# An LSTM with a sign-weight FFN: x's last quarter and Wx as scaled pairs of f16

## The chip, the cores and the metric

The kernel runs on one core of a Trainium2 chip. The metric is the device time of one execution in microseconds (us), the median of three runs.

## What is computed

An LSTM over 64 steps with 32 sequences and 256 features, and a three-layer network whose weights are only +1 or -1, on all 2048 outputs of the LSTM, added to x:

```python
xW = einsum('ntd,dg->ntg', x, Wx) + b          # x: 32 x 64 x 256, Wx: 256 x 1024
def step(h, c, xw_t):                          # 64 times
    a = xw_t + h @ Wh                          # 32 x 1024
    i, f, o = sigmoid(three quarters of a); g = tanh(last quarter)
    c = f * c + i * g
    h = o * tanh(c)
z = concatenate([hs, -hs], -1)                 # 2048 x 512
z = relu(s0 * z @ W0) * 2                      # W0: 512 x 1024 of +1/-1
z = relu(s1 * z @ W1) * 2                      # W1: 1024 x 1024 of +1/-1
out = x + s2 * z @ W2                          # W2: 1024 x 256 of +1/-1
```

## The kernel before

**Number formats.** A product of two fp32 operands is made from halves. For x @ Wx each operand is split into a value rounded to the matmul's rounded fp32 and the rest (`xs`, `wxs`), and three of the four products are summed: 6 matmuls of 128 x 128 x 512 for one tile of xW. h and Wh are pairs of f16, scaled by powers of two that are taken from the largest value; FFN weights are exact 8-bit floats, and activations are pairs of f16.

**x @ Wx.** Four quarters i of 512 columns (16 steps x 32 sequences), eight tiles j of 128 gates: the tiles `("x", i, j)`, or x0/0 to x3/7. x0 comes before the loop, x1 begins before it. In the loop, x's quarters 2 and 3 are rounded by ScalarE (`x_hi`, in steps 1, 2 and 4, 5) and their rests are made by VectorE (`x_lo`, at the ends of steps 1, 2 and 4, 5). ScalarE's `x_empty` copies a finished tile from PSUM to `xw` and adds the bias.

**The loop.** TensorE starts step t with 32 matmuls of Wh's low half (L508) and 32 of its high half (L517). VectorE sums their halves (`tensor_reduce`, L1033), ScalarE takes tanh, VectorE makes vT (L1039), uT, cD, ScalarE tanh of c, and VectorE h: the high half, the fp32 value, and the low half (L1053, semaphore `hl_made`). ScalarE also seeds PSUM with the next step's xW.

**Fill.** Behind the gate matmuls TensorE does the work of `pe_plan[t]`: tiles of x, layer 0 `(0, c, m)`, layer 1 `(1, c, m)`, output `("o", c, k)`, and for the last two chunks seven products `p1` to `p7` in place of eight. `make_plan` writes the whole order out ahead of time, from one list of tiles (`tile_order`). A step gets a credit, the fill, and pays for each matmul until 0.1 us or less is left; a tile whose inputs or whose PSUM bank aren't there in the plan's reckoning ends the step:

```python
return 3.4 if t < 0 else 1.8 if t < 1 else 2.3 if t < 9 else 2.2 if t < 16 else 2.3   # fill(t)
return 0.229 if tile[0] == "x" else 0.000422 * width(tile)                             # cost(tile)
credit = min(credit, 1.0) + fill(t)
while piece < len(order) and credit > 0.1:
```

Four PSUM banks take the tiles in turn (`free.pop(0)`), and `wait_empty` makes a tile's first matmul wait for the tile that had its bank. Tiles are emptied by ScalarE (high half, L718, or `x_empty`, L693) and VectorE (low half, L872) in the order of `act_plan[t]` and `dve_plan[t]`, which run once the h of step t is on its way, so around the start of step t+1. Within `act_plan[t]` x tiles come last (`act[t].sort(key=lambda x: (x[0] == "y", x[0] == "x"))`). VectorE's other chores (`x_lo`, `w0_make`, `w1_make`, `w2_make`) come between the low half of h and these. In plan steps with an x tile, TensorE does the x matmuls behind the others.

**GpSimd.** Before the loop one maximum over partitions and the casts of x's second quarter. In the loop its chores of `pool_plan[t]` wait for `hl_made` t+1: sums of W1's quarters (`mix_part`, L1111), `r1_rest` (L1131), `y_add` (L1125). The planner gives a step chores of at most 1.3 us.

**The end.** After the loop (plan step 64) come the rest of the output tiles, layer 0 of the last chunk, which needs h of step 63, and the products.

## Time and profile before

| | |
|---|---|
| median of 3 runs | 273.12 us (273.04 to 273.39) |
| profiled execution | 273.06 us, its span 271.20 us |
| TensorE matmuls | 267.2 us busy, 99% of the span, 3568 of them |
| weight loads | 219.9 us |
| VectorE | 215.4 us, 79% |
| ScalarE | 174.6 us, 64% |
| GpSimd | 48.1 us, 18% |
| TensorE's granted clock | 1.0 of full speed over the span |

The span is cut from the profiled execution's own time; the rest lies around it. PE is TensorE's matmuls, PEld its weight loads, DVE VectorE, ACT ScalarE, POOL GpSimd. A busy TensorE is not a TensorE at its peak: the ends of matmuls are modelled, and waits inside a row of matmuls may not show. A line number is that of the kernel before.

### The profile page before, as it was taken

To read this page: it belongs to the slowest core of one execution; us is meant where nothing else is said; L and a number is where in the kernel's file an instruction comes from. 1 tells how busy PE (TensorE), PEld (TensorE's weight loads), DVE (VectorE), ACT (ScalarE), POOL (GpSimd) and SP (SyncE) were. 2 spreads that over 40 slices of the span, in tenths; PEclk is the share of its full clock that TensorE was granted. 3 is DMA by queue.
4 is the path that set the end of the run, shared out by engine and by line. 5 is a ranking of instruction groups with operands and counts; after the bars stand their busy time and mean duration, and the time that the engine had idled before them with its cause. 6 is when DMAs were issued, how large, how long until landed. Compare 5 with 4: busy or idle time off the path is not lost.

```text
span 271.2 us, 8903 instructions
## 1 busy us (share of the span) xinstructions
PE 267.2 (99%) x3568; PEld 219.9 (81%) x3568; DVE 215.4 (79%) x769; ACT 174.6 (64%) x522; POOL 48.1 (18%) x70
## 2 busy tenths in 40 slices
PE   8999999999999999999999999999999999999995
PEld 6888888878999999999998899998887676666563
DVE  3878888888888888888888888887777777997355
ACT  4789786878566667655765576556777867733320
POOL 0010000012211112331222102000222225603030
PEclk9999999999999999999999999999999999999999
DMA  7980000000000000000010001000000010100003
GB/s 210 346 342 1 4 2 0 2 4 2 2 0 4 4 2 22 22 2 5 2 42 0 2 4 41 2 2 4 4 0 2 2 42 0 41 0 0 2 0 116
DMA packets 5432, 8.72 MB, mean 32 GB/s; under 512 B 656, under 2 KB 3472, under 8 KB 5264
## 3 DMA queue, kind: packets, MB, share of 16 engines
q1 hardware_dynamic: 5104, 7.64, 8.1%
q8 instruction: 28, 0.46, 0.7%
q10 hardware_dynamic: 288, 0.52, 0.5%
q14 instruction: 12, 0.10, 0.1%
HBM read 6.07 MB, written 2.10 MB: 30 GB/s over the span
## 4 chain that ended last, share of the span: by engine, by line
PE 98%; DVE 1%; POOL 0%; issue 0%; POOLq 0%
PE WK L555 36%; PE WK L538 14%; PE G L517 11%; PE WK L573 10%; PE G L508 10%; PE ACC L587 6%; PE G L573 4%; PE WK L604 2%; PE ACC L604 1%; PE G L649 1%; PE G L538 1%; PE ACC L538 1%; DVE x L886 1%; PE G L555 0%; POOL zero L1094 0%
## 5 line engine op out<-in xcount | busy, mean ns | idle before, releaser
L555 PE MATMUL WK<-h,k 128*128 128x256 f16 (+1 forms) x856 | 107.7, 276 | 0.0
L555 PEld LDWEIGHTS WK<-h,k 128*128 128x128 fp8e5 x856 | 80.8, 98 | 11.3 <-issue 0.2
L814 ACT ACTIVATE tT<-aT 128x128 f32<-128x128 f32 x126 | 39.0, 310 | 44.6 <-DVE aT L1033 43.4
L1033 DVE TENSOR_REDUCE aT<-G 128x128 f32<-128x256 f32 x128 | 48.2, 418 | 7.7 <-PE G L517 6.3
L701 ACT ACTIVATE G<-xw 128x256 f32<-128x256 f32 x126 | 46.6, 370 | 0.0
L538 PE MATMUL WK<-xs,wxs 128*128 128x512 f32 x168 | 42.5, 400 | 0.0
L517 PE MATMUL G<-h,w 128*128 128x64 f16 x1008 | 39.5, 192 | 0.0
L508 PEld LDWEIGHTS G<-h,w 128*128 128x128 f16 x1008 | 32.9, 96 | 6.7 <-DVE h L1050 5.1
L538 PEld LDWEIGHTS WK<-xs,wxs 128*128 128x128 f32 x168 | 30.4, 188 | 5.9
L508 PE MATMUL G<-h,w 128*128 128x32 f16 x1008 | 35.2, 177 | 0.0
L517 PEld LDWEIGHTS G<-h,w 128*128 128x128 f16 x1008 | 33.2, 97 | 0.0
L872 DVE SCALAR_TENSOR_TENSOR h<-WK,h 128x256 f16<-128x256 f32 x80 | 30.9, 418 | 0.0
L819 ACT ACTIVATE tC<-cD 128x64 f32<-128x64 f32 x64 | 16.4, 256 | 17.5 <-DVE cD L1044 17.5
L718 ACT ACTIVATE h<-WK 128x256 f16<-128x256 f32 x80 | 26.6, 368 | 0.0
L1050 DVE TENSOR_TENSOR h<-oP,tC 128x64 f16<-128x64 f32 x64 | 14.4, 225 | 14.2 <-ACT tC L819 14.2
L1111 POOL TENSOR_TENSOR mix<-k 128x256 fp8e5<-128x256 fp8e5 x16 | 10.3, 648 | 71.4 <-DVE h L1053 71.4
L587 PE MATMUL ACC<-h,k 128*128 128x256 f16 x160 | 22.0, 273 | 0.0
L1042 DVE SCALAR_TENSOR_TENSOR uT<-tT,cD 128x64 f32<-128x64 f32 x63 | 14.2, 225 | 6.6
L693 ACT ACTIVATE xw<-WK,biasS 128x512 f32<-128x512 f32 x28 | 18.0, 676 | 0.6 <-PE WK L538 0.6
L587 PEld LDWEIGHTS ACC<-h,k 128*128 128x128 fp8e5 x160 | 15.3, 98 | 2.1
L573 PE MATMUL WK<-xw,k 128*128 128x384 f16 x96 | 16.7, 326 | 0.0
L1039 DVE SCALAR_TENSOR_TENSOR vT<-tT 128x64 f32<-128x64 f32 x63 | 14.2, 225 | 2.9
(116 smaller groups left out, 283.9 us busy)
## 6 DMA issues: line engine op xcount, KB each, us to landing
x<-in_x SPq DMA_DIRECT2D x3, 512.0 KB, 8.4
out_y<-x SPq DMA_DIRECT2D x10, 128.0 KB, 1.8
...
```

What stands on the lines that cost most here:

```text
L508: eng.matmul(G[g][:, 64 * (j - j0):64 * (j - j0) + B], w16[:, 1, j, k], hi[:, k], start=False, stop=False, skip_group_check=True)
L517: ins = eng.matmul(G[g][:, 64 * (j - j0):64 * (j - j0 + 1)], w16[:, 0, j, k], pair[:, k].rearrange("p a b -> p (a b)"), start=False, stop= ...
L538: ins = eng.matmul(TILE[bank[tile]][:, :], wxs[:, wp, k, j], xs[:, i % 2, xp, k], start=a == 0, stop=a == 5)
L555: ins = eng.matmul(layer_src(tile), w, rhs, start=a == 0, stop=last)
L573: ins = eng.matmul(layer_src(tile), w[:, k, 128 * m:128 * m + 128], rhs[:, k, part], start=a == 0 and q not in (2, 6, 7), stop=a == 7, ski ...
L587: ins = eng.matmul(ACC[mo][:, 0:width(tile)], w2[:, k, 128 * mo:128 * mo + 128], h2[:, k, part, 0:width(tile)], start=k == 0 and part == 0 ...
L693: eng.activation(xw[:, 4 * i:4 * i + 4, j], TILE[bank[tile]][:, :].rearrange("p (u c) -> p u c", c=128), ACT.Identity, bias=biasS[:, j:j + ...
L701: eng.activation(G[g][:, 0:256].rearrange("p (j h b) -> p j h b", h=2, b=B), src.unsqueeze(2).broadcast_to((P, 4, 2, B)), ACT.Copy, scale= ...
L718: eng.activation(layer_dst(tile, 0), layer_src(tile), ACT.Relu).then_inc(hi_made[layer])
L814: eng.activation(tT[:, B * j0:B * j1], aT[:, j0:j1].rearrange("p j b -> p (j b)"), ACT.Tanh, scale=half_gain0 if t == 0 else half_gain).th ...
L872: eng.scalar_tensor_tensor(layer_dst(tile, 1), layer_src(tile), 0.0, layer_dst(tile, 0), ALU.max, ALU.subtract).then_inc(lo_made[tile[0]])
L1033: eng.tensor_reduce(aT[:, j0:j1], G[g][:, 0:256].rearrange("p (j h b) -> p j b h", h=2, b=B), op=ALU.add, axis=AX.X).then_inc(added[g])
```

## The change

- **x's last quarter and Wx as f16 pairs.** The 48 matmuls of x3 read `wx16` and `x3p`, pairs of f16, both scaled by powers of two; `x_empty` scales back. The matmuls of x0, x1 and x2 stay as they are.
- **Scales.** VectorE takes four maxima over Wx in its prologue (`wx_max`) and two over x's last quarter in steps 0 and 1 (`x3_max`), with two small ones behind the second; GpSimd takes the maximum over partitions (`x3_max_all`), and VectorE makes the scales in step 2 (`x3_scale`).
- **The parts.** GpSimd scales Wx in place (`wx_scale`), makes its high parts (`wx16_hi`) and rests (`wx16_lo`) half by half, and x's high part (`x3_hi`); VectorE makes x's rest (`x3_lo`) in steps 6 and 7.
- **x's third quarter.** ScalarE rounds it before the loop and in step 0, GpSimd makes its rest (`x2_lo`) in steps 0 and 2.
- **Other chores.** `w0_make` moves from steps 0, 3, 6 to 2, 3, 4; `w1_make` from two parts of 1024 columns in steps 7 and 8 to four of 512 in steps 5, 5, 8, 10. The sums of W1's quarters start in step 12 instead of 10.
- **The plan.** An x3 matmul costs 0.216 instead of 0.229; x3 is ready in step 9 instead of 6 and stands further back among layer 0's first tiles; x3's matmuls are no longer put behind the others of their step. `fill` and the credit rule stay.

```diff
--- before.py
+++ after.py
@@ -43,16 +43,24 @@
 WX_GROUPS = ((0, 1, 0, 2), (0, 1, 2, 4), (1, 2, 0, 2), (1, 2, 2, 4), (0, 2, 4, 6), (0, 2, 6, 8))
 
 
-X2_STEPS = (1, 2)
-X3_STEPS = (4, 5)
-W0_STEPS = (0, 3, 6)
-W1_STEPS = (7, 8)
+X3_MAX_STEPS = (0, 1)
+X3_SCALE_STEP = 2
+X3_LO_STEPS = (6, 7)
+W0_STEPS = (2, 3, 4)
+W1_STEPS = (5, 5, 8, 10)
 W2_STEPS = (15,)
 
+
+X3_CHORES = {0: (("x2_lo", 0),), 1: (("x3_max",),), 2: (("x2_lo", 1),), 3: (("wx_scale", 0, 0), ("wx_scale", 1, 0)),
+             4: (("wx16_hi", 0, 0), ("wx16_hi", 1, 0)), 5: (("x3_hi", 0), ("x3_hi", 1)), 6: (("wx16_lo", 0, 0),),
+             7: (("wx16_lo", 1, 0),), 8: (("wx_scale", 0, 1), ("wx_scale", 1, 1)), 9: (("wx16_hi", 0, 1), ("wx16_hi", 1, 1)),
+             10: (("wx16_lo", 0, 1),), 11: (("wx16_lo", 1, 1),)}
+X3_READY = 9
...
-MIX_STEP, MIXES = 10, 32
+MIX_STEP, MIXES = 12, 32
 CHORES, EVICTIONS = 1.3, 1.7
...
 def cost(tile):
-    return 0.229 if tile[0] == "x" else 0.000422 * width(tile)
+    return (0.216 if tile[1] == 3 else 0.229) if tile[0] == "x" else 0.000422 * width(tile)
...
     for m in range(8):
-        order += [(("x", 3, n), 6) for n in range(NJ) if (0, 1, 2, 3, 4, 5, 6, 8)[n] == m] + [((0, 0, m), 4)]
+        order += [(("x", 3, n), 6) for n in range(NJ) if (3, 3, 4, 5, 5, 6, 7, 8)[n] == m] + [((0, 0, m), 4)]
...
         if tile[0] == "x":
-            inputs = t >= (-1, -1, 3, 6)[tile[1]]
+            inputs = t >= (-1, -1, 3, X3_READY)[tile[1]]
...
-        if 0 <= t and any(tile[0] == "x" for tile, _ in pe[t]):
-
-            pe[t].sort(key=lambda p: p[0][0] == "x")
+        if 0 <= t and any(tile[0] == "x" and tile[1] < 3 for tile, _ in pe[t]):
+
+            pe[t].sort(key=lambda p: p[0][0] == "x" and p[0][1] < 3)
             ends = list(accumulate(cost(tile) for tile, _ in pe[t]))
             finished = [(tile, at) for (tile, a), at in zip(pe[t], ends) if a + 1 == matmuls(tile)]
...
+        pool[t] += X3_CHORES.get(t, ())
         chores.sort(key=lambda x: (x[0] != 0, x[0] == "mix"))
-        while chores and 0 <= t < T and sum(map(pool_cost, pool[t] + chores[:1])) <= CHORES:
+        while chores and t not in X3_CHORES and 0 <= t < T and sum(map(pool_cost, pool[t] + chores[:1])) <= CHORES:
             pool[t].append(chores.pop(0))
...
-            time = ahead + STEP + spent - CHAIN - KEEP - LOW * (t in W2_STEPS)
+            time = ahead + STEP + spent - CHAIN - KEEP - LOW * (t in W2_STEPS + W1_STEPS)
...
+        wx16 = cut(h1[:, 1], 0, 2, 2, NJ, 128)
+        x3p = cut(h1[:, 1], 4 * NJ * 128, 2, 2, 512)
...
+                if i == 3:
+                    e.wait_ge(wx16l if wp else wx16h, 2 * (j // 4) + k + 1)
+                    e.wait_ge(x3l if xp else x3h, k + 1)
+                    ins = eng.matmul(TILE[bank[tile]][:, :], wx16[:, wp, k, j], x3p[:, xp, k], start=a == 0, stop=a == 5)
+                    if a == 5:
+                        ins.then_inc(x_mm)
+                    return
...
-                if xp:
+                if xp and i == 2:
+                    e.wait_ge(xl2, k + 1)
+                elif xp:
...
-                    e.wait_ge(w1_made, 2)
+                    e.wait_ge(w1_made, len(W1_STEPS))
...
+                    e.wait_ge(wx16l, 2 * (j // 4) + 2)
+                    gain = descale2 if j < 2 else descale
+                else:
+                    gain = 2.0 if j < 2 else 1.0
                 eng.activation(xw[:, 4 * i:4 * i + 4, j], TILE[bank[tile]][:, :].rearrange("p (u c) -> p u c", c=128),
-                               ACT.Identity, bias=biasS[:, j:j + 1], scale=2.0 if j < 2 else 1.0).then_inc(x_out)
+                               ACT.Identity, bias=biasS[:, j:j + 1], scale=gain).then_inc(x_out)
...
+                if layer == 0 and c == 1:
+                    e.wait_ge(x_mm, 4 * NJ)
...
                 x_empty(tile)
+            x_hi(2, 0)
...
-                if t + 1 in X2_STEPS:
-                    x_hi(2, X2_STEPS.index(t + 1))
-                if t + 1 in X3_STEPS:
-                    x_hi(3, X3_STEPS.index(t + 1))
+                if t == 0:
+                    x_hi(2, 1)
                 for tile in act_plan[t]:
                     empty(tile)
...
+            def wx_max(n):
+
+                for g in ((0, 1), (2, 3), (4, 5), (4, 5))[n]:
+                    e.wait_ge(dwx[g], 16)
+                eng.tensor_reduce(mxx[:, n:n + 1], wx[:, n % 2, 4 * (n // 2):4 * (n // 2) + 4].rearrange("p j c -> p (j c)"),
+                                  op=ALU.max, axis=AX.X, apply_absolute_value=True).then_inc(x_maxed)
+
+            def x3_max(k):
+                e.wait_ge(dx[2], 16)
+                eng.tensor_reduce(mxx[:, 5 + k:6 + k], x[:, k, 1536:2048], op=ALU.max, axis=AX.X,
+                                  apply_absolute_value=True).then_inc(x_maxed)
+                if k == 1:
+                    e.wait_ge(guarded, 2)
+                    e.wait_ge(x_maxed, 6)
+                    eng.tensor_reduce(mxx[:, 8:9], mxx[:, 0:5], op=ALU.max, axis=AX.X).then_inc(x_maxed)
+                    eng.tensor_reduce(mxx[:, 9:10], mxx[:, 5:8], op=ALU.max, axis=AX.X).then_inc(x_maxed)
+
+            def x3_lo(k):
+                e.wait_ge(x3h, k + 1)
+                eng.scalar_tensor_tensor(x3p[:, 1, k], x[:, k, 1536:2048], scale_x3, x3p[:, 0, k], ALU.mult,
+                                         ALU.subtract).then_inc(x3l)
+
+            def x3_scale():
+
+                e.wait_ge(x_max_all, 1)
+                eng.tensor_scalar(scx[:, 0:2], max2x[:, :].bitcast(I32), 0x7F800000, None, ALU.bitwise_and).then_inc(x_scaled)
+                e.wait_ge(x_scaled, 1)
+                eng.tensor_scalar(scx[:, 2:4], scx[:, 0:2], -1.0, float(267 << 23), ALU.mult, ALU.add).then_inc(x_scaled)
+                for n, add in ((4, 153), (5, 152)):
+                    eng.scalar_tensor_tensor(scx[:, n:n + 1], scx[:, 0:1], float(-(add << 23)), scx[:, 1:2], ALU.add,
+                                             ALU.add).then_inc(x_scaled)
...
             def w1_make(n):
-                part = k1[:, 1024 * n:1024 * n + 1024]
+                part = k1[:, 512 * n:512 * n + 512]
                 e.wait_ge(dk1, 16)
                 eng.tensor_scalar(part, part, seven[:, :], sign1[:, :], ALU.logical_shift_left,
...
+            wx_max(0)
             wx_lo(4)
...
+            wx_max(1)
             wx_lo(5)
...
+            wx_max(2)
             x_lo(1, 0)
             w_lo(0)
             x_lo(1, 1)
...
+            wx_max(3)
             signs()
...
-                if t in X2_STEPS:
-                    x_lo(2, X2_STEPS.index(t))
-                if t in X3_STEPS:
-                    x_lo(3, X3_STEPS.index(t))
+                if t in X3_MAX_STEPS:
+                    x3_max(X3_MAX_STEPS.index(t))
+                if t == X3_SCALE_STEP:
+                    x3_scale()
+                if t in X3_LO_STEPS:
+                    x3_lo(X3_LO_STEPS.index(t))
                 if t in W0_STEPS:
                     w0_make(W0_STEPS.index(t))
-                if t in W1_STEPS:
-                    w1_make(W1_STEPS.index(t))
+                for n in range(len(W1_STEPS)):
+                    if W1_STEPS[n] == t:
+                        w1_make(n)
...
+            def x2_lo(k):
+                eng.wait_ge(xh, 2 + k)
+                eng.tensor_tensor(xs[:, 0, 1, k, :], x[:, k, 1024:1536], xs[:, 0, 0, k, :].bitcast(F32),
+                                  ALU.subtract).then_inc(xl2)
+
+            def x3_max_all():
+                eng.wait_ge(x_maxed, 8)
+                eng.partition_all_reduce(max2x[:, :], mxx[:, 8:10], P, bass.bass_isa.ReduceOp.max).then_inc(x_max_all)
+
+            def wx16_parts(k, half):
+                js = slice(4 * half, 4 * half + 4)
+                return (v.rearrange("p j c -> p (j c)") for v in (wx[:, k, js], wx16[:, 0, k, js], wx16[:, 1, k, js]))
+
+            def wx_scale(k, half):
+
+                src, hi, lo = wx16_parts(k, half)
+                eng.wait_ge(x_scaled, 2)
+                eng.wait_ge(wxl, len(WX_GROUPS))
+                eng.tensor_scalar(src, src, scale_wx, None, ALU.mult).then_inc(wxs16)
+
+            def wx16_hi(k, half):
+                src, hi, lo = wx16_parts(k, half)
+                eng.wait_ge(wxs16, 2 * half + k + 1)
+                eng.tensor_copy(hi, src).then_inc(wx16h)
+
+            def wx16_lo(k, half):
+                src, hi, lo = wx16_parts(k, half)
+                eng.wait_ge(wx16h, 2 * half + k + 1)
+                eng.tensor_tensor(lo, src, hi, ALU.subtract).then_inc(wx16l)
+
+            def x3_hi(k):
+                eng.wait_ge(x_scaled, 2)
+                eng.tensor_scalar(x3p[:, 0, k], x[:, k, 1536:2048], scale_x3, None, ALU.mult).then_inc(x3h)
...
             for t in range(T):
                 if pool_plan[t]:
                     eng.wait_ge(hl_made, t + 1)
                 for chore in pool_plan[t]:
-                    if chore[0] == "mix":
+                    if chore[0] == "x2_lo":
+                        x2_lo(chore[1])
...
```

## Rows read from the trace of the kernel before

**Rows 1.** The page's shares of the chain that ended last, by engine.

```profile
PE 98%; DVE 1%; POOL 0%; issue 0%; POOLq 0%
```

**Rows 2.** That chain in order of time: start us, length us, work.

```profile
10.42 8.84 PE WK L538 x39
...
71.03 2.40 PE WK L555 x22
```

**Rows 3.** TensorE's timeline, steps 2 to 15: start us, us, engine, line, work.

```profile
25.28 0.57 PE L508 MATMUL G<-h,w 128*128 128x32 f16 x16
...
44.94 0.57 PE L508 MATMUL G<-h,w 128*128 128x32 f16 x16
...
54.45 0.56 PE L508 MATMUL G<-h,w 128*128 128x32 f16 x16
...
57.51 0.56 PE L508 MATMUL G<-h,w 128*128 128x32 f16 x16
...
66.88 0.56 PE L508 MATMUL G<-h,w 128*128 128x32 f16 x16
```

**Rows 4.** The timeline of step 11 on all engines; in brackets idle time and releaser.

```profile
54.49 0.22 DVE L1053 TENSOR_TENSOR h<-h 128x64 f16<-128x64 f32 x1
...
54.68 0.42 DVE L872 SCALAR_TENSOR_TENSOR h<-WK,h 128x256 f16<-128x256 f32 x1
...
54.81 0.64 POOL L1111 TENSOR_TENSOR mix<-k 128x256 fp8e5<-128x256 fp8e5 x1 [40.12 <-DVE h L1053]
...
55.29 0.75 DVE L1033 TENSOR_REDUCE aT<-G 128x128 f32<-128x256 f32 x2 [0.19 <-PE G L517]
...
55.32 0.60 PE L555 MATMUL WK<-h,k 128*128 128x256 f16 x4
...
56.09 0.23 DVE L1039 SCALAR_TENSOR_TENSOR vT<-tT 128x64 f32<-128x64 f32 x1
...
57.41 0.37 ACT L718 ACTIVATE h<-WK 128x256 f16<-128x256 f32 x1
...
57.62 0.22 DVE L1053 TENSOR_TENSOR h<-h 128x64 f16<-128x64 f32 x1
...
57.67 0.68 ACT L693 ACTIVATE xw<-WK,biasS 128x512 f32<-128x512 f32 x1
```

**Rows 5.** The timeline of the loop's last step and what follows it.

```profile
220.21 0.55 PE L508 MATMUL G<-h,w 128*128 128x32 f16 x16
...
221.37 0.74 DVE L1033 TENSOR_REDUCE aT<-G 128x128 f32<-128x256 f32 x2
...
224.06 1.46 PE L555 MATMUL WK<-h,k 128*128 128x384 f16 x8
```

**Rows 6.** Groups by line and shape: busy us, mean ns, idle before.

```profile
L857 DVE TENSOR_REDUCE mx<-xw 128x1 f32<-128x512 f32 x4 | 2.5, 677 | 0.0
...
L1125 POOL TENSOR_TENSOR x<-x,t1f 128x256 f32<-128x256 f32 x8 | 5.8, 730 | 25.9 <-DVE h L1053 25.9
...
L1131 POOL TENSOR_TENSOR xw<-xw 128x384 f16<-128x384 f32 x8 | 7.3, 915 | 40.8 <-DVE h L1053 36.2 <-ACT xw L712 4.6
...
L971 DVE TENSOR_SCALAR k<-k,seven,sign 128x512 uint32<-128x512 uint32 x1 | 0.5, 541 | 0.0
```

**Rows 7.** Timeline of the prologue, and L1120's durations (min/median/max ns).

```profile
13.51 1.18 POOL L1101 CAST xs<-x 128x512 fp32r<-128x512 f32 x2 [1.22 <-DMA x<-in_x]
...
14.16 1.07 DVE L867 TENSOR_TENSOR xs<-x,xs 128x512 fp32r<-128x512 f32 x1 [0.65 <-POOL xs L1101]
...
15.81 0.68 DVE L867 TENSOR_TENSOR xs<-x,xs 128x512 fp32r<-128x512 f32 x1
...
L1120 POOL TENSOR_TENSOR w<-xw,h x4: 1020/1022/1419, 227.7 to 235.4; 128x384 f32<-128x384 f32 x4
```

**Rows 8.** Timeline of VectorE, small operations and the first reduce.

```profile
12.86 0.40 DVE L1015 TENSOR_SCALAR sci<-sci 128x1 int32<-128x1 int32 x5
...
20.05 0.76 DVE L1033 TENSOR_REDUCE aT<-G 128x128 f32<-128x256 f32 x2 [0.72 <-PE G L517]
```

More of the change, by code:

```diff
@@ L315, in lstm_ffn @@
         sci = sb("sci", [P, 10], I32)
+        mxx = sb("mxx", [P, 10], F32)
+        max2x = sb("max2x", [P, 2], F32)
+        scx = sb("scx", [P, 6], I32)
         hz = sb("hz", [P, 2, 2, B], F16)
@@ L386, in lstm_ffn @@
         FAC = sc[:, 15:16]
+        scale_wx, scale_x3, descale, descale2 = (scx[:, n:n + 1].bitcast(F32) for n in (2, 3, 4, 5))
         dwh = [sem(f"dwh{g}") for g in range(4)]
@@ L396, in lstm_ffn @@
         wxh, wxl, whi, wlo, xh, xl = (sem(n) for n in ("wxh", "wxl", "whi", "wlo", "xh", "xl"))
-        xh0, xh1 = sem("xh0"), sem("xh1")
+        xh0, xh1, xl2 = sem("xh0"), sem("xh1"), sem("xl2")
+        guarded, x_maxed, x_max_all, x_scaled = (sem(n) for n in ("guarded", "x_maxed", "x_max_all", "x_scaled"))
+        wxs16, wx16h, wx16l, x3h, x3l = (sem(n) for n in ("wxs16", "wx16h", "wx16l", "x3h", "x3l"))
         zeroed, maxed, max_all, scaled, biased, signed, hz_hi, hz_lo = (
@@ L1096, in _ @@
             eng.memset(seven[:, :], 7).then_inc(zeroed)
+            eng.memset(mxx[:, 4:5], 2.0 ** -33).then_inc(guarded)
+            eng.memset(mxx[:, 7:8], 2.0 ** -67).then_inc(guarded)
             eng.wait_ge(maxed, 7)
@@ L1136, in _ @@
                 for chore in pool_plan[t]:
-                    if chore[0] == "mix":
+                    if chore[0] == "x2_lo":
+                        x2_lo(chore[1])
+                    elif chore[0] == "x3_max":
+                        x3_max_all()
+                    elif chore[0] == "wx16_hi":
+                        wx16_hi(chore[1], chore[2])
+                    elif chore[0] == "wx16_lo":
+                        wx16_lo(chore[1], chore[2])
+                    elif chore[0] == "x3_hi":
+                        x3_hi(chore[1])
+                    elif chore[0] == "wx_scale":
+                        wx_scale(chore[1], chore[2])
+                    elif chore[0] == "mix":
                         mix_part(chore[1])
```

4 lines of the change are left out of this document (2 added, 2 removed).

## The prediction

> **What bounds the kernel now.** I read four views in this order. The chain of work that ended last comes first: 98% of it is TensorE [rows 1]. The same chain piece by piece gives the pace. 39 matmuls of 512 rounded-fp32 columns take 8.84 us, 227 ns each, and 22 matmuls of 256 f16 columns take 2.40 us, 109 ns each [rows 2]. Then the timeline of TensorE. Call T(n) the start of the first gate matmul (L508) of loop step n. T(2) is 25.28 and T(8) is 44.94, so six steps of ten x matmuls last 3.28 us each. T(8) to T(15) is 21.94 us: 3.17 for each of steps 8 to 10 (9.51 to T(11) at 54.45), 9.37 for steps 12 to 14, and step 11, with little extra work, lasts 3.06 us [rows 3]. Last, step 11 on all engines [rows 4]: DVE's reduce (L1033) starts at T+0.84, the low half of h (L1053) starts 2.33 us after it, and the next T lies 0.11 before that low half when TensorE waits for the recurrence. So a step costs the larger of two: the 64 gate matmuls, 0.88 us (in step 11 the fill starts at T+0.87 [rows 4]), plus its fill; and the recurrence, 0.84 + 2.33 - 0.11 = 3.06. Whatever pushes the reduce, or blocks a DVE operation after it, lengthens the second. Steps of ten x matmuls have 0.22 to spare, steps 8 to 14 at most some 0.1. TensorE works strictly in the planned order: a fill matmul that waits holds up the next step's gates too.
>
> **What f16 removes.** 48 of the 144 x matmuls in the loop's plan change. The planner's 0.422 ns per column, which the 109 ns row bears out, gives 216 ns instead of 227: 48 x 0.011 = 0.5 us. The planner charges 0.216 for 0.229 and so brings 0.62 us, six 256-column matmuls, forward. Steps 15 to 62 stay as full as they were, so this comes back only where the loop ends. There it meets a floor: the first matmul of the last chunk needs the low half of h(63). That starts 2.33 after the reduce at 221.37, at 223.70, takes 0.22, and the matmul starts at 224.06 [rows 5]. With four product matmuls fewer ahead of it, it can start earlier only as far as h does. The last reduce is late today, T+1.16, and that 0.3 goes if its product is out a step earlier. I take a gain of 0.4 (0 to 0.65).
>
> **What is hidden.** Four maxima over Wx are added to DVE's prologue, 0.68 each [rows 6]. Three fall ahead of the x subtraction of 14.16, which has 0.65 of idle time before it and is held until 14.69 by GpSimd's casts anyway [rows 7]; the last one has the 0.72 idle ahead of the first reduce at 20.05 [rows 8]. Cost 0; if the cover fails, 0.6. The rounding of x's third quarter moves on ScalarE to before step 0, where that same wait hides it. No DMA moves.
>
> **The shared SBUF path.** GpSimd did nothing between its casts and step 11, 40.12 us [rows 4]; now it has chores in plan steps 0 to 11. A DVE subtraction with two SBUF inputs takes 0.68 at 15.81 and took 1.07 at 14.16, beside GpSimd's second cast, which ran to 14.69; it ended 0.54 after that cast. On the other side, GpSimd's subtraction of 1.02 took up to 1.42 [rows 7]. So I let one wait for the end of the other. "SBUF — State Buffer" of the Trainium skill, in its part on the two sides of SBUF, says that the pair of ports is an exclusive lock for the whole instruction, against DVE operations with two SBUF inputs or in a two-port mode. The rows agree with it, as far as they go. By the lock the collisions below add about 1.9 us; by a flat 0.4 a collision, as the rows lengthened, about 0.9.
>
> GpSimd starts 0.32 after the start of h's low half [rows 4]: at T+0.4 in steps that wait for the recurrence, and at T+0.2 in full ones, where that half starts up to 0.2 earlier against T. Its durations: one input, 512 columns: 0.59 to 0.61 a cast. Two inputs: 0.73 for 256 and 1.02 for 384 columns, so 1.31 for 512; with f16 out 0.92 for 384, so 1.21 [rows 6, 7]. A scale by a pointer has no row; I take the cast's 0.61, and up to 1.31 as the bound. The operations behind the reduce have two SBUF inputs, the first of them (vT) 0.80 after it, at T+1.64 [rows 4].
>
> Step by step against the times before (DVE's chores of plan step t run at the start of step t+1, and so do GpSimd's):
> - Step 3: DVE has four tiny scale operations (five take 0.40 [rows 8], and one waits for the first: ready at T+0.46), then w0_make(0), two inputs, 0.62 (0.68 with its end, as the subtraction of 15.81 [rows 7]). GpSimd's x2_lo(1) has been running since T+0.20, to T+1.51. w0_make ends at 2.13, and the reduce starts 1.29 late: 2.13 + 2.33 - 0.11 = 4.35, +1.07. If DVE got in first, vT would wait instead: +0.1.
> - Step 6: two w1_make of 0.45 (0.54 with its ends [rows 6]) and two x3_hi on GpSimd. DVE first: +0.28; alternating: +0.54. I take +0.35. Steps 4 and 7: vT waits 0.26 and 0.29, of which 0.22 is spare: +0.11 together. Steps 1, 2, 5: within the spare time.
> - Step 8: x3_lo to T+0.72, then wx16_lo to T+1.93; vT is due at 1.64, so 3.06 + 0.29 = 3.35 against 3.17: +0.18.
>
> **The plan of steps 8 to 14.** It follows from the code. Credit at step 8 is 2.303. x2/7 takes 0.687 and the layer tiles 0, 1 and 2 take 1.296; x3 is not ready; 0.320 is left. Step 9 (+2.2): x3/0 and x3/1, 12 x 0.216. Step 10 (2.128): layer tile 3, x3/2, and three matmuls of tile 4. Step 11 (2.275): the last of tile 4, x3/3, and the first four of x3/4. Step 12: two of x3/4, tile 5, x3/5. Step 13: tile 6, x3/6, tile 7. Step 14: x3/7 and nine of layer 1 (three before). Two waits follow.
> - Step 9: x3/0 gets the bank of x2/7. ScalarE evicts three layer tiles ahead of it, because x tiles are sorted last. It starts at T-0.10, takes 0.27 a tile and 0.68 for x [rows 4]: done at T+1.39, where TensorE asks at T+0.88. With the hand-over 1.43 + 12 x 0.2155 = 4.02, with the boundary 4.05 against 3.17: +0.88. If the bank were free in time, the recurrence still has w1_make and two evictions (0.35 apiece, 0.42 with its ends) ahead of a reduce at T+1.41, so 3.63: +0.46.
> - Step 11: the fourth matmul of x3/4 reads wx16_lo(1,1), GpSimd's chore of plan step 11, and that waits for hl_made 12, which step 11's own recurrence makes. w1_make and one eviction start the reduce at T+1.10, h's low half starts at 3.43, GpSimd at 3.75, done 4.96. TensorE wanted it at T+2.93. It resumes at 5.0 with the last fill matmul, and the gates of step 12 start at T+5.25 against 3.06: +2.19. Queued behind the waiting matmul are those gates, and behind them DVE, ScalarE and all of the recurrence. No cover. Bounds: 1.6 (GpSimd at a cast's speed) to 2.5.
> - Steps 10, 12 and 13 run at 3.06 and step 14 at 3.16, 12.34 together against 3.17 + 9.37 = 12.54 before: -0.20.
>
> Sum: 1.07 + 0.35 + 0.11 + 0.18 + 0.88 + 2.19 - 0.20 = 4.58, less 0.4 at the end of the loop: +4.2. The profiled execution took 273.06 us (span 271.20), 0.06 under the median of 273.12. That gives **277.3**.
>
> **Rivals.**
> 1. The engines do not block each other in the loop. Steps 3, 4, 6, 7, 8 lose only what order costs, and step 11 starts its reduce the same: 4.2 less about 1.9 gives 275.4. For it: step 11 has a mix part on GpSimd and the shortest recurrence there is. Against it: there GpSimd is done before vT [rows 4]. It decides at step 3.
> 2. The stall of step 11 is missing, since the matmul falls in step 12 or GpSimd gets its half in time: 277.3 - 2.1 = 275.2. Against it: only a credit off by 0.12 us changes the plan, and the GpSimd chore can't start before step 11's h.
> 3. Other side: every part is ready before TensorE asks. It decides where wx16_lo(1,1) is ready by T(11)+2.93 and DVE's new work ends by T+0.84. What is left is the matmul saving, at most 0.5 to 0.65: 272.5. For it: TensorE is 98% of the chain and GpSimd is idle in these steps. Against it: the order just worked out.
> 4. GpSimd's scales cost 1.31 each: two of them run past vT in step 4, x3_hi likewise in step 6, and wx_scale in step 9 delays the recurrence behind TensorE's own wait. 0.8 + 0.8 + 0.3 more: 279.2.
>
> **How the numbers follow.** Forecast 0.55, rival 1 0.15, rival 2 0.10, rival 3 0.08, rival 4 0.08; 0.04 for small losses that just balance the saving. So faster by over 0.2% 0.08, within 0.2% 0.04, slower 0.88 (0.2% is about what a measurement of this kernel can tell from no change). The range takes in rivals 1 and 2 below and the upper bounds of steps 9 and 11 above: 275.0 to 279.0.
>
> **What would show it.** In the trace after: T(2) unchanged at about 25.3; a step 3 of some 4.4 us with w0_make stretched to over 1 us; x matmuls of x3 at 216 ns; a gap of half a microsecond ahead of x3/0 in step 9, released by ScalarE's eviction; a gap of two microseconds in step 11, released by GpSimd's subtraction; steps from 15 on as before; the first matmul of the last chunk 0.1 to 0.5 us earlier relative to T(63). The prediction is wrong if the planned order differs from the one above, if GpSimd's part is ready sooner than 0.3 after h's low half plus its own time, or if DVE and GpSimd run side by side.

## The result

The changed kernel takes 285.78 us (284.83 to 287.24, 4 runs) against 273.14 (273.04 to 273.39, 4 runs) for the kernel before: ratio 1.0457, 95% interval 1.0436 to 1.0478. The forecast was 277.3 with a range up to 279.0. The direction was right; the loss, 12.6 us, is three times as large as forecast. Of what the forecast missed, 7.3 us are in steps 3 to 5 of the profiled execution, as the table below shows. The profiled execution of the changed kernel took 284.83 us, its span 283.0, against 273.06 and 271.2. The forms of the tables are those of before; line numbers are now those of the changed kernel (gate matmuls L526 and L535, x matmuls L565, x3's f16 matmuls L551, layer tiles L582).

The page of after: share of the chain by engine, and from the 40 slices the rows of TensorE, GpSimd and the granted clock.

```profile
PE 69%; DVE 8%; issue 5%; ACT 3%; POOL 3%; POOLq 0%; DVEq 0%
...
PE   8999749997999999999999999999999999999995
...
POOL 0011074663111211232123212000222312713030
PEclk9999968999999999999999999999999999999999
```

TensorE's share of the chain fell from 98% [rows 1] to 69%. One slice is 7 us. TensorE's row dips to 7 and 4 in slices 5 and 6 (28 to 42 us), and the clock's row in slices 6 and 7 (35 to 50 us). The loss is early in the loop. TensorE's timeline says in which steps:

```profile
25.64 0.57 PE L526 MATMUL G<-h,w 128*128 128x32 f16 x16
26.51 2.54 PE L565 MATMUL WK<-xs,wxs 128*128 128x512 f32 x10
29.00 0.57 PE L526 MATMUL G<-h,w 128*128 128x32 f16 x16
...
33.88 0.57 PE L526 MATMUL G<-h,w 128*128 128x32 f16 x16 [1.46 <-DVE h L1118]
...
39.05 4.64 PE L565 MATMUL WK<-xs,wxs 128*128 128x512 f32 x10 [4.14 <-POOL xs L1208]
...
43.49 0.65 PE L526 MATMUL G<-h,w 128*128 128x32 f16 x16
...
58.90 2.76 PE L551 MATMUL WK<-h 128*128 128x512 f16 x12 [0.40 <-ACT xw L724]
...
69.43 0.39 PE L551 MATMUL WK<-h 128*128 128x512 f16 x1 [1.79 <-POOL h L1234]
...
78.98 0.55 PE L526 MATMUL G<-h,w 128*128 128x32 f16 x16
...
232.28 0.55 PE L526 MATMUL G<-h,w 128*128 128x32 f16 x16
```

T(2) is 25.64 (25.28 in [rows 3]), T(3) 29.00, T(4) 33.88, T(5) 43.49, T(15) 78.98 (66.88 in [rows 3]), T(63) 232.28 (220.21 in [rows 5]). In the same way for every step:

| part | before, us | after, us | difference | forecast |
|---|---|---|---|---|
| T(0), then steps 0 to 2 | 28.56 | 29.00 | +0.44 | 0 |
| step 3 | 3.28 | 4.88 | +1.60 | +1.07 |
| step 4 | 3.27 | 9.61 | **+6.34** | +0.05 |
| step 5 | 3.28 | 3.73 | +0.45 | 0 |
| step 6 | 3.27 | 3.91 | +0.64 | +0.35 |
| step 7 | 3.28 | 3.26 | -0.02 | +0.06 |
| step 8 | 3.17 | 3.06 | -0.11 | +0.18 |
| step 9 | 3.17 | 4.05 | +0.88 | +0.88 |
| step 11 | 3.06 | 5.11 | +2.05 | +2.19 |
| steps 10, 12, 13, 14 | 12.54 | 12.37 | -0.17 | -0.20 |
| steps 15 to 62 | 153.33 | 153.30 | -0.03 | 0 |
| from T(63) to the end | 50.99 | 50.72 | -0.27 | -0.4 |
| span | 271.2 | 283.0 | +11.8 | +4.2 |

(Steps 4 and 7 had one term, +0.11, in the forecast. Of the +0.44 of the first row 0.31 is T(0), 19.41 against 19.10, no more than kernels with one prologue differ among themselves: y1_f16_only, y3_f16_cost and p1_probe, whose prologue is that of before, have 19.48, 19.71 and 19.75.) Now the same steps on GpSimd and VectorE, from the timeline of after:

```profile
23.17 1.28 POOL L1208 TENSOR_TENSOR xs<-x,xs 128x512 fp32r<-128x512 f32 x1 [8.03 <-ACT xs L711]
...
26.72 0.15 DVE L907 TENSOR_REDUCE mxx<-mxx 128x1 f32<-128x3 f32 x1
...
30.23 0.37 POOL L1213 PARTITION_ALL_REDUCE max2x<-mxx  x1 [5.78 <-DVE h L1121]
...
30.64 0.17 DVE L917 TENSOR_SCALAR scx<-max2x 128x2 int32<-128x2 int32 x1 [1.31 <-POOL max2x L1213]
...
37.28 1.72 POOL L1208 TENSOR_TENSOR xs<-x,xs 128x512 fp32r<-128x512 f32 x1 [6.68 <-DVE h L1121]
39.00 3.14 POOL L1224 TENSOR_SCALAR xw<-xw,scx 128x512 f32<-128x512 f32 x2
```

Read it along GpSimd. `x2_lo(0)` ends at 24.45. The last input of the partition maximum (L1213) is there at 26.87, its operation stands at 30.23: 5.78 idle from the end of the one to the start of the other, 3.36 of them after everything it waits for was done. So `x3_scale` on VectorE starts at 30.64, in front of `w0_make(0)` and the reduce, and step 3 ends 1.60 late. Then GpSimd is idle for another 6.68 us ahead of `x2_lo(1)`. The view names h's low half (L1121) as what ended it, but that h, step 2's, was done at 29.33. GpSimd waited for nothing that the trace shows. TensorE wants `x2_lo(1)` in step 4 and gets it at 39.0, after 4.14 us without a matmul; 0.44 of them are the subtraction itself, 1.72 long beside a VectorE operation, where `x2_lo(0)` took 1.28. What follows is in the windows (busy time by engine, and behind them the granted clock):

```profile
core 0: us, PE busy (x) PEld busy (x) DVE busy (x) ACT busy (x) POOL busy (x), PEclk, DMA share, GB/s
20.00:29.00 9.00, 9.00 (x109) 7.01 (x105) 7.56 (x31) 6.81 (x21) 1.28 (x1) 1.00 0.02 6
29.00:39.00 10.00, 4.46 (x75) 3.58 (x74) 6.58 (x27) 4.60 (x13) 2.09 (x3) 0.95 0.01 2
39.00:44.00 5.00, 4.95 (x27) 3.65 (x28) 0.00 (x0) 1.38 (x2) 4.26 (x5) 0.50 0.00 0
44.00:51.10 7.10, 6.64 (x74) 5.28 (x70) 5.82 (x19) 4.29 (x13) 3.34 (x2) 0.94 0.01 2
```

The granted clock is 0.50 from 39 to 44 us, the 1.2 GHz level. The ten x matmuls of step 4 take 4.64 us where ten of step 2 took 2.54: 2.1 us on top. Wait and clock, 4.14 + 2.1, are the 6.34 of step 4 to 0.1. Step 5 still begins at that level: its gates take from 43.49 to the fill at 44.81, 1.32 for 0.87, and that is all of its +0.45. The clock fell while TensorE still stood: its gates end at 34.92, the granted clock is 1.00 up to 38 us, 0.53 from 38 to 39 and 0.50 up to 44. The clock also tells the runs of this kernel apart: over the whole span it is 0.988 in the one of 284.83 and 0.982 in the other three, 285.34 to 287.24.

### The profile page after: what moved, and what is told of

Its sections match the earlier page's. It is cut to its first block, busy times and chain, and to the rows that moved or that the text cites. A ratio compares the mean times of both kernels' runs of the same rounds, so it can differ in the third digit from the quotient of the medians.

```text
span 283.0 us, 8958 instructions
## 1 busy us (share of the span) xinstructions
PE 270.0 (95%) x3568; PEld 217.9 (77%) x3568; DVE 220.6 (78%) x781; ACT 174.6 (62%) x520; POOL 69.4 (25%) x89
## 4 chain that ended last, share of the span: by engine, by line
PE 69%; DVE 8%; issue 5%; ACT 3%; POOL 3%; POOLq 0%; DVEq 0%
PE WK L582 32%; PE G L535 8%; PE G L526 7%; PE WK L600 6%; PE ACC L614 6%; PE G L600 4%; ACT tT L848 2%; PE WK L631 2%; PE WK L551 2%; PE WK L565 2%; DVE aT L1101 2%; PE ACC L631 1%; POOL xw L1204 1%; DVE uT L1110 1%; POOL h L1234 1%
## 5 line engine op out<-in xcount | busy, mean ns | idle before, releaser
L582 PE MATMUL WK<-h,k 128*128 128x256 f16 (+1 forms) x856 | 107.4, 276 | 0.3 <-DVE h L1121 0.3
L582 PEld LDWEIGHTS WK<-h,k 128*128 128x128 fp8e5 x856 | 80.8, 98 | 12.7 <-issue 0.5
L535 PE MATMUL G<-h,w 128*128 128x64 f16 x1008 | 39.9, 193 | 0.0
L526 PEld LDWEIGHTS G<-h,w 128*128 128x128 f16 x1008 | 33.2, 96 | 8.6 <-DVE h L1118 5.7
L526 PE MATMUL G<-h,w 128*128 128x32 f16 x1008 | 35.2, 177 | 2.0 <-DVE h L1118 2.0
L565 PE MATMUL WK<-xs,wxs 128*128 128x512 f32 x120 | 32.2, 419 | 4.2 <-POOL xs L1208 4.1
L535 PEld LDWEIGHTS G<-h,w 128*128 128x128 f16 x1008 | 33.6, 98 | 0.0
L565 PEld LDWEIGHTS WK<-xs,wxs 128*128 128x128 f32 x120 | 23.2, 200 | 9.4 <-POOL xs L1208 4.3
L1107 DVE SCALAR_TENSOR_TENSOR vT<-tT 128x64 f32<-128x64 f32 x63 | 15.1, 240 | 3.3 <-ACT tT L848 0.6
L724 ACT ACTIVATE xw<-WK,biasS 128x512 f32<-128x512 f32 x20 | 13.0, 677 | 5.4 <-PE WK L565 5.4
```

The source lines that it names most:

```text
L526: eng.matmul(G[g][:, 64 * (j - j0):64 * (j - j0) + B], w16[:, 1, j, k], hi[:, k], start=False, stop=False, skip_group_check=True)
L535: ins = eng.matmul(G[g][:, 64 * (j - j0):64 * (j - j0 + 1)], w16[:, 0, j, k], pair[:, k].rearrange("p a b -> p (a b)"), start=False, stop= ...
L565: ins = eng.matmul(TILE[bank[tile]][:, :], wxs[:, wp, k, j], xs[:, i % 2, xp, k], start=a == 0, stop=a == 5)
L582: ins = eng.matmul(layer_src(tile), w, rhs, start=a == 0, stop=last)
```

## The experiments

**Is the gap the maximum's own? p1_probe.** Into the kernel before, five small operations on scratch data that nobody reads, in GpSimd's step 1:

```diff
             for t in range(T):
+                if t == 1:
+                    eng.wait_ge(hl_made, 2)
+                    eng.tensor_tensor(probe[:, 0], h16[:, 0, 0].rearrange("p a b -> p (a b)"), h16[:, 0, 1].rearrange("p a b -> p (a b)"), ALU.add)
+                    eng.partition_all_reduce(probe[:, 1, 0:2], mx[:, 6:8], P, bass.bass_isa.ReduceOp.max)
+                    eng.tensor_copy(probe[:, 2], h16[:, 0, 0].rearrange("p a b -> p (a b)"))
+                    eng.tensor_tensor(probe[:, 3], h16[:, 0, 0].rearrange("p a b -> p (a b)"), h16[:, 0, 1].rearrange("p a b -> p (a b)"), ALU.add)
+                    eng.tensor_scalar(probe[:, 4], h16[:, 0, 0].rearrange("p a b -> p (a b)"), FAC, None, ALU.mult)
```

> The kernel before with five extra GpSimd operations behind the low half of h of step 1, on small data that nothing reads: a sum, a maximum over partitions, a cast, a sum, a scale. Theory B (the maximum came late in the changed kernel because it waited for VectorE's maxima or for the SBUF path): all five run back to back, gaps under 0.5 us.

273.69 us (1 run), beside 273.65 (273.06 to 274.03, 7 runs) for the kernel before on that chip. GpSimd's timeline:

```profile
26.17 0.67 POOL L1137 TENSOR_TENSOR probe<-h 128x64 f32<-128x64 f16 x1 [11.60 <-DVE h L1054]
32.82 0.46 POOL L1138 PARTITION_ALL_REDUCE probe<-mx  x1 [5.98 <-issue]
33.16 0.30 POOL L1139 CAST probe<-h 128x64 f32<-128x64 f16 x1
40.48 0.30 POOL L1140 TENSOR_TENSOR probe<-h 128x64 f32<-128x64 f16 x1 [7.02 <-issue]
40.79 0.45 POOL L1141 TENSOR_SCALAR probe<-h,sc 128x64 f32<-128x64 f16 x1
```

With inputs that had long been there the maximum has 5.98 us of nothing ahead of it, and the next subtraction or addition 7.02, while the cast between them starts at once. Both gaps come with the maximum. Nobody waits here, and the time doesn't change: the gap costs only whoever waits for GpSimd. "GPSIMD Engine Reference" of the Trainium skill, section 2.1 on dispatch, says that the first call of a freshly loaded routine pays about 6 us for loading its code, without an instruction in the profile. The first gap agrees in size. But the same operation had already run once in this kernel, before the loop, so the gap is not confined to its first call; of the second gap the page says nothing. That either gap is the loading of code is therefore argued, not shown.

**Take the maximum out: x1_fixed_scale.** The changed kernel with constant scales: two small fills stand in the place of the maximum over partitions. VectorE's maxima are still made, but not used.

```diff
-                eng.partition_all_reduce(max2x[:, :], mxx[:, 8:10], P, bass.bass_isa.ReduceOp.max).then_inc(x_max_all)
+                eng.memset(max2x[:, 0:1], 0.25)
+                eng.memset(max2x[:, 1:2], 4.0).then_inc(x_max_all)
```

> The changed kernel with the two scales fixed (two small fills on GpSimd in place of the maximum over partitions; the maxima on VectorE stay, but what they find isn't used). Theory A: steps 3 and 4 fall from 4.88 and 9.61 us to between 3.3 and 4.4 each, TensorE's clock stays up, 285.8 becomes 277 to 279. Theory B: the late start of x2_lo(1) has another cause, and the kernel stays above 283. My prediction's collision (w0_make against x2_lo(1) in step 3) would show here undisturbed: 4.35 us for step 3, about 3.3 if the two can overlap.

279.97 us (277.49 to 280.03, 4 runs), ratio 1.0203, interval 1.0152 to 1.0255. Step 3 is 4.59 and step 4 is 3.41. Without the gaps the forecast's own collision shows, from the timeline:

```profile
29.69 1.29 POOL L1208 TENSOR_TENSOR xs<-x,xs 128x512 fp32r<-128x512 f32 x1 [2.30 <-DVE scx L917]
29.72 1.28 DVE L919 TENSOR_SCALAR scx<-scx 128x2 int32<-128x2 int32 x1
```

A scale operation of two columns, 0.17 long in the changed kernel, takes 1.28 and ends with GpSimd's subtraction. The forecast named the operation behind it, `w0_make(0)`; the reduce starts at 31.65, 2.38 after T(3). Steps 6, 9 and 11 are 4.03, 4.04 and 5.10. Step 12 is 4.72 in the profiled run. The windows of steps 11 and 12, columns as above:

```profile
57.95:63.05 5.10, 3.31 (x44) 1.92 (x44) 3.50 (x14) 3.33 (x9) 2.54 (x2) 1.00 0.00 2
63.05:67.77 4.72, 4.72 (x46) 2.54 (x45) 2.51 (x10) 2.40 (x7) 0.64 (x1) 0.64 0.01 3
```

Its granted clock was 0.64, behind the 1.8 us that TensorE stands in step 11 (busy 3.31 of 5.10); in the changed kernel, behind the same gap, step 12 is 3.05. So the gap of step 11 costs 2 us, and the clock behind it took 1.7 more in step 12 of this execution. The run of 277.49 has a granted clock of 1.0 over its span, the three around 280 have 0.994; what the rest of the 2.5 between them is, the one profile can't say.

**The order of x3's products: a1_order and x2_fixed_order.** The changed kernel, and x1_fixed_scale, with the two products of Wx's low part last in each x3 tile:

```diff
                 if i == 3:
+                    k, wp, xp = ((0, 0, 0), (1, 0, 0), (0, 0, 1), (1, 0, 1), (0, 1, 0), (1, 1, 0))[a]
```

> The changed kernel with one edit: in the x3 tiles the two products with Wx's low part come last, so the fourth matmul of x3/4 doesn't read GpSimd's last piece. If the gap of 1.79 us in step 11 is that wait alone: step 11 falls from 5.11 to 3.1 us, the kernel by 2.0 us to 283.8. If it only moves (the fifth and sixth matmul wait in step 12), under 1 us.

> Both edits: fixed scales and the low products last. If the two costs add: x1 less 2.0 us, 275 to 277. Then 2 to 4 us over the kernel before are left, in steps 3 to 9.

a1_order takes 283.33 (283.10 to 283.57, 4 runs), ratio 1.0357 (1.0336 to 1.0377): step 11 falls from 5.11 to 3.26, step 12 rises from 3.05 to 3.58, since the matmul that needs `wx16_lo(1,1)` is now in step 12 and waits 0.4. Steps 3 and 4 stay at 4.70 and 9.52. x2_fixed_order takes 276.88 (276.21 to 277.99, 4 runs), ratio 1.0123 (1.0088 to 1.0158), and no step loses clock. The stall of step 11 is `wx16_lo(1,1)`, as forecast, and it is independent of what the maximum costs. These two kernels differ in the maximum alone, and that gives its price here: 283.33 less 276.88, 6.45 us, of which 6.11 in step 4 of the profiles (9.52 against 3.41). It is less than the 8.4 us that steps 3 to 5 of the changed kernel are over before: without the late maximum the collision takes 1.3 in step 3, and a1_order's step 5, at 3.25, loses no clock.

**The maximum behind x2_lo(1): m1_reduce_last.** The changed kernel, with GpSimd's two chores exchanged, so that TensorE need not wait for `x2_lo(1)`:

```diff
-X3_CHORES = {0: (("x2_lo", 0),), 1: (("x3_max",),), 2: (("x2_lo", 1),), 3: (("wx_scale", 0, 0), ("wx_scale", 1, 0)),
+X3_CHORES = {0: (("x2_lo", 0),), 1: (("x2_lo", 1), ("x3_max",)), 3: (("wx_scale", 0, 0), ("wx_scale", 1, 0)),
```

> The changed kernel with one edit: GpSimd makes the second half of x2's rest in plan step 1, ahead of the maximum over partitions, instead of in plan step 2 behind it. 
A miss: 283.99 (282.91 to 284.95, 4 runs), ratio 1.0411 (1.0389 to 1.0433). From the timeline:

```profile
32.79 0.37 POOL L1213 PARTITION_ALL_REDUCE max2x<-mxx  x1 [5.75 <-issue]
33.20 0.17 DVE L917 TENSOR_SCALAR scx<-max2x 128x2 int32<-128x2 int32 x1 [4.13 <-POOL max2x L1213]
...
36.44 0.61 PE L526 MATMUL G<-h,w 128*128 128x32 f16 x16 [4.31 <-DVE h L1118]
...
40.76 3.12 POOL L1224 TENSOR_SCALAR xw<-xw,scx 128x512 f32<-128x512 f32 x2 [7.60 <-DVE h L1121]
```

The gap went from one waiting engine to another. VectorE now waits 4.13 for the scales ahead of the reduce, the recurrence stops, and TensorE is without work for 4.31 instead of 4.14. Step 3 is 7.71; step 4, at a granted clock of 0.66 over its 4.5 us, is 4.49, where 3.4 was expected; step 6 is 4.63, for 3.91 in the changed kernel. The second gap, 7.60, now stands ahead of the scaling of Wx: it isn't the subtraction alone that has it.

**The shared path: x3_lo_early.** x2_fixed_order with that same exchange; with constant scales no gap comes into it, and the subtraction no longer meets the scale operations of step 3.

> Fixed scales, low products last, and x2_lo(1) in plan step 1, where VectorE has no operation with two SBUF inputs at that moment. If step 3's 4.57 us are the collision of w0_make(0) with x2_lo(1): step 3 falls to 3.3 to 3.4 us, the kernel from 276.9 to 275.7. If they are x3_scale's own length: step 3 stays above 4.

275.97 (275.34 to 276.09, 4 runs), ratio 1.0101 (1.0081 to 1.0120). Step 3 falls from 4.57 to 3.48; the others stay within 0.02. 1.1 us of step 3 was the collision.

**GpSimd's scaling of x: x4_all.** x3_lo_early with x's high part made by ScalarE in steps 3 and 4. (A second edit, a new sorting key for ScalarE's evictions, left their order as it was, so the eviction of x2/7 was not tested here.)

```diff
-             4: (("wx16_hi", 0, 0), ("wx16_hi", 1, 0)), 5: (("x3_hi", 0), ("x3_hi", 1)), 6: (("wx16_lo", 0, 0),),
+             4: (("wx16_hi", 0, 0), ("wx16_hi", 1, 0)), 6: (("wx16_lo", 0, 0),),
...
+                if t in (3, 4):
+                    x3_hi(t - 3)
```

> As the one before, and two more edits: ScalarE evicts x2/7 ahead of step 8's layer tiles, and x3's high part is made on ScalarE instead of GpSimd. If each of the rest of the forecast's waits is what it was taken for: step 9 falls from 4.04 to 3.5 to 3.7 us (the recurrence behind w1_make and two evictions), step 6 from 4.03 to 3.3 to 3.4; the kernel 275.7 less 1.1 = 274.6, still 0.5 to 1 us over the kernel before. If the f16 matmuls bring their 0.5 us on top of that, 274.0; if the kernel comes below 273.2, the gain of f16 is larger than 0.5.

274.88 (274.57 to 275.10, 5 runs), ratio 1.0066 (1.0051 to 1.0081). Step 6 falls from 4.03 to 3.26: 0.77 us were GpSimd's two `x3_hi` against VectorE's `w1_make` and vT. Step 9 stays at 4.04.

**Bank and chores: x5_more.** x4_all with x2/7 evicted first, `wx16_lo` of the second half one plan step earlier, `w1_make` in steps 5, 5, 9, 10.

```diff
-        act[t].sort(key=lambda x: (x[0] == "y", x[0] == "x" and x != ("x", 2, 7)))
+        act[t].sort(key=lambda x: (x[0] == "y", -1 if x == ("x", 2, 7) else x[0] == "x"))
...
-             10: (("wx16_lo", 0, 1),), 11: (("wx16_lo", 1, 1),)}
+             10: (("wx16_lo", 0, 1), ("wx16_lo", 1, 1)), 11: ()}
```

> The kernel of x4_all (fixed scales, new product order, x2_lo(1) earlier, x's high part on ScalarE) with three more moves: ScalarE evicts x2/7 ahead of the layer tiles of its step, wx16_lo of the second half is one plan step earlier, and w1_make stands in steps 5, 5, 9, 10. If the 0.9 us of step 9 are the bank of x2/7 behind three evictions, step 9 falls from 4.04 to about 3.5 (the recurrence then sets it), and step 12 from 3.59 to about 3.1: about 273.8 in all. If step 9 is long for another reason, it stays at 4.0 and only step 12 gains: 274.4.

A miss: 274.96 (274.63 to 275.40, 5 runs), ratio 1.0062 (1.0048 to 1.0076), no better than x4_all. From its timeline:

```profile
49.44 2.75 PE L552 MATMUL WK<-h 128*128 128x512 f16 x12
49.58 0.76 DVE L943 SCALAR_TENSOR_TENSOR h<-WK,h 128x256 f16<-128x256 f32 x2 [0.68 <-ACT h L752]
50.25 0.75 DVE L1108 TENSOR_REDUCE aT<-G 128x128 f32<-128x256 f32 x2
...
56.22 2.50 POOL L1242 TENSOR_TENSOR h<-xw,h 128x512 f16<-128x512 f32 x2 [1.86 <-DVE h L1128]
...
57.63 1.18 DVE L1114 SCALAR_TENSOR_TENSOR vT<-tT 128x64 f32<-128x64 f32 x1
```

TensorE's wait for the bank is gone, but the layer tiles' high halves now come later from ScalarE, VectorE waits 0.68 for them, and the reduce starts 1.69 after T(9): step 9 is 3.98 by the recurrence. Step 12 fell to 3.07, step 10 rose from 3.06 to 3.26 and step 11 from 3.25 to 4.01: two subtractions of GpSimd in a row hold vT for 1.18 instead of 0.23. Both waits that were moved here landed on the other path.

**What f16 is worth: y1_f16_only and y3_f16_cost.** The kernel before with x3's 48 matmuls on f16 data that are in SBUF anyway (xW of the last quarter is then not the reference's), once with the plan as it was, once with the price of 0.216.

```diff
+                if i == 3:
+                    e.wait_ge(wlo, 4)
+                    ins = eng.matmul(TILE[bank[tile]][:, :], w16[:, wp, j, k], w16[:, xp, 4 * k:4 * k + 2].rearrange(FLAT), start=a == 0, stop=a == 5)
```

> The kernel before, with x3's 48 matmuls on f16 data that are in SBUF already (Wh's parts as weights and as moving data; xW of the last 16 steps is not the reference's) and the plan as it was. It measures the matmul saving alone. Theory: 48 x 0.011 = 0.5 us less, part of it lost where a step already waits for the recurrence, so 0.2 to 0.5 less than before. Rival: an f16 matmul of 512 columns, with its weight load, costs the same as the rounded fp32 one here: no difference. Other rival: the f16 matmul gains more than 11 ns: over 0.6 less.

> y1_f16_only with the planner's price of an x3 matmul at 0.216 in place of 0.229, so that 0.6 us of later matmuls come forward. Theory of the prediction: the gain shows where the loop ends, 0.4 us (0 to 0.65) less than before. Rival: it is lost at the recurrence's floor in steps 8 to 14 and at the end, and the time is that of before within 0.2%.

y1_f16_only: 273.09 (272.79 to 273.70, 11 runs), ratio 0.9998 (0.9989 to 1.0007). y3_f16_cost: 273.26 (272.99 to 273.69, 11 runs), ratio 0.9991 (0.9982 to 1.0000). Before: 273.27 (21 runs). In y1 T(8) to T(15) shrinks by 0.24 us (21.70 against 21.94), the other steps stay. In y3 the end after T(63) is 50.71 instead of 50.99, and step 61 is 3.42 instead of 3.14: the work that the plan brings forward is paid for where the recurrence has no room, 0.28 for 0.28. T(8) to T(15) is 22.21 in y3, 0.27 more than before: its step 14 takes 3.45.

**The real maximum, with nobody waiting: x6_real_scale.** x4_all with the maximum back, the scales made in step 4, and the chores behind it moved to where GpSimd is ready again:

```diff
-X3_SCALE_STEP = 2
+X3_SCALE_STEP = 4
...
+X3_CHORES = {0: (("x2_lo", 0),), 1: (("x2_lo", 1), ("x3_max",)), 5: (("wx_scale", 0, 0), ("wx_scale", 1, 0)),
+             6: (("wx16_hi", 0, 0), ("wx16_hi", 1, 0)), 7: (("wx16_lo", 0, 0),), 8: (("wx16_lo", 1, 0), ("wx_scale", 0, 1)),
+             9: (("wx_scale", 1, 1), ("wx16_hi", 0, 1), ("wx16_hi", 1, 1)), 10: (("wx16_lo", 0, 1),), 11: (("wx16_lo", 1, 1),)}
...
-                if t in (3, 4):
-                    x3_hi(t - 3)
+                if t in (5, 6):
+                    x3_hi(t - 5)
...
-                eng.memset(max2x[:, 0:1], 0.25)
-                eng.memset(max2x[:, 1:2], 4.0).then_inc(x_max_all)
+                eng.partition_all_reduce(max2x[:, :], mxx[:, 8:10], P, bass.bass_isa.ReduceOp.max).then_inc(x_max_all)
```

> The kernel of x4_all with the real maximum over partitions in place of the constants, so with both 6 to 7 us gaps on GpSimd, but nobody waits for it in them: both x2_lo come before it, the scales are made in step 4 instead of 2, GpSimd's first scale of Wx is in plan step 5, its other chores are two steps later or closer together, and ScalarE makes x's high part in steps 5 and 6. Theory: after's 8 us are only the two waits and the clock that falls behind them. Then the two gaps stand in GpSimd's row as before, step 3 is 3.3, step 4 3.3 to 3.5, step 5 about 3.5, the granted clock is 1.0, and the time is 275.0 to 276.3. Rival: fetching the code costs TensorE or VectorE something by itself, or the later chores of GpSimd run into steps 7 to 12 and block vT in each: over 278.

276.16 (275.85 to 276.31, 4 runs), ratio 1.0104 (1.0087 to 1.0121). From the timeline:

```profile
33.26 0.37 POOL L1219 PARTITION_ALL_REDUCE max2x<-mxx  x1 [5.84 <-issue]
...
35.68 0.17 DVE L923 TENSOR_SCALAR scx<-max2x 128x2 int32<-128x2 int32 x1
...
41.10 3.13 POOL L1230 TENSOR_SCALAR xw<-xw,scx 128x512 f32<-128x512 f32 x2 [7.47 <-issue]
```

Both gaps are there, 5.84 and 7.47, and nobody waits for GpSimd in them. Steps 3, 4 and 5 are 3.24, 3.26 and 3.31, and the granted clock is 1.0 over the span in all four runs. Against the changed kernel 9.6 us are gone with the same sums of the same parts, in another order and with x's high part made by ScalarE. Not all of it is the waiting: a1_order, with the same maximum and the same order of products, takes 283.33, 7.2 more, and of these ScalarE's part is worth up to 1.1 (x3_lo_early against x4_all). The 1.3 us over x4_all are in steps 6, 7 and 10 (3.80, 3.72, 3.57 against 3.26, 3.26, 3.06), less 0.25 in step 3: GpSimd's chores, now closer together, run beside VectorE's recurrence there; in step 7, for one, vT takes 0.63 instead of 0.23. It beats the changed kernel, not the one before.

## Why the prediction was wrong

1. **What failed: the term that isn't there.** `x3_max_all` stands in the list of changes, and the sum has no price for it, neither for its duration nor for what is queued behind it; the steps of GpSimd were all costed as if the engine were free at T+0.2. So two waits were missing: 3.36 us between the maximum's inputs and its start, and 6.68 us ahead of `x2_lo(1)`, which put 4.14 us without a matmul into a step that was forecast at +0.05. Shown by p1_probe (the gaps stand alone), x1_fixed_scale (without it step 4 is 3.41), a1_order against x2_fixed_order (6.45 us between them) and x6_real_scale (with it, and no waiting engine, step 4 is 3.26). The trace of before had one such maximum, before the loop, where its inputs come so late that no gap can be seen; it gave no bound from above, and the forecast should have said so and made a rival of it.
2. **The clock, 2.1 us in step 4 and 0.45 in step 5, follows from it.** There was no term for it, and the longest wait of the forecast was 2.1 us. What sets off the fall wasn't in any row of before, whose granted clock is 1.0 over the span. The wait of 4.14 was followed by a granted clock of 0.50 for 5 us, that of 4.31 in m1_reduce_last by 0.66 over step 4. In a1_order it fell earlier in the same wait (0.88 from 35 to 37 us, 0.50 to 43), and step 5 is 3.25. The gap of step 11 did it in x1_fixed_scale's profile and not in the changed kernel's: what tells these two apart stays open.
3. **Step 3: right in the mechanism, hidden in the result.** The changed kernel's +1.60 is the late maximum; there `x2_lo(1)` ran only after step 3 and met nothing in it. The collision that the forecast describes came out in x1_fixed_scale, 4.59 against 4.35 forecast, and went in x3_lo_early (3.48). The blocked operation was a scale operation, not `w0_make(0)`.
4. **Step 6 and GpSimd's scaling: a term mis-sized.** It was costed at a cast's 0.61, with 1.31 as bound. The groups by line and shape of after say:

```profile
L1224 POOL TENSOR_SCALAR xw<-xw,scx 128x512 f32<-128x512 f32 x4 | 6.5, 1643 | 1.6 <-DVE h L1121 1.6
...
L1238 POOL TENSOR_SCALAR h<-x,scx 128x512 f16<-128x512 f32 x2 | 3.3, 1678 | 4.1 <-DVE h L1121 4.1
...
L1229 POOL CAST h<-xw 128x512 f16<-128x512 f32 x4 | 2.3, 614 | 0.4 <-DVE h L1121 0.4
```

   1.64 to 1.68 us each, outside the range. It cost step 6 0.64 instead of 0.35 (0.75 in x1_fixed_scale, which is the 0.8 of rival 4); in steps 4 and 9, where rival 4 saw 0.8 and 0.3 more, nothing came of it (3.41 and 4.04 in x1_fixed_scale).
5. **Step 5** lost 0.45 to the clock alone; x1_fixed_scale has 3.24 there. **Step 8** was costed with GpSimd's subtraction against vT, +0.18, and has 3.06: vT is 0.33 long there for 0.23, and ends at 56.36, 0.08 behind the subtraction. The meeting took place, but uT starts at 56.37, 0.34 after vT's start, and it starts 0.33 after it where nothing meets (27.57 and 27.90). So the longer vT cost the step nothing.
6. **Step 9, +0.88, and step 11, +2.05,** came as worked out, from ScalarE's late eviction of x2/7 (0.40 of wait) and from `wx16_lo(1,1)`, done 69.38, 1.79 of wait. a1_order shows the second; x5_more shows that even without the first, and with `w1_make` moved out of the step, the recurrence keeps it at 3.98 (3.63 forecast for that case).
7. **The gain of f16, 0.4, was too high.** 0.27 came at the end, 0.03 before it; y1 and y3 put the whole of it, without any preparation, at 0.02% and 0.09%, within 0.2% of nothing.
8. **The rest held:** no cost of the prologue that can be told from chance (T(0) is 19.20 to 19.74 in kernels with the change, 19.10 to 19.75 in those without it), steps 10 and 12 to 14, the plan's order, steps 15 to 62, and the first matmul of the last chunk, 0.31 earlier against T(63). Step 2, which was to stay within its spare time, took 0.08 more: the small maxima start its reduce at T+1.14, and by the forecast's own rule 1.14 + 2.33 - 0.11 is 3.36, as measured. Leave the maximum out and the forecast is close, partly by luck, since step 6 cost more and steps 8 and 11 less: x1_fixed_scale's profile, counted from T(0), is 6.2 us over before, 4.5 without the clock's 1.7, for +4.2. Its one run at full clock is 3.8 over before (277.49 against 273.65), but x2_fixed_order's four runs alone spread by 1.8.
